# Attention stage of a four-layer graph network: pairs of 512-column tiles cast and subtracted as one, accumulators read behind the subtraction, degrees in three batches, drains replaced by semaphores

## The reference

```python
deg = jnp.clip(adj.sum(axis=1), 1.0)
dis = deg ** (-0.5)
adj_norm = dis[:, None] * adj * dis[None, :]
diffusion = adj_norm @ x - x
norms = jnp.maximum(jnp.linalg.norm(x, axis=-1), COS_EPS)
sim = x @ x.T / (norms[:, None] * norms[None, :])
attn = jax.nn.softmax(beta * sim * adj, axis=1)
return diffusion + jax.nn.sigmoid(alpha) * (attn @ x - x)
```

## Time and profile before

| | |
|---|---|
| median of 3 runs | 945.01 us (944.57 to 945.73) |
| profiled execution | 945.11 us, of which the span of its instructions 943.3 us |
| PE busy | 856.4 us (91%) |
| DVE busy | 642.5 us (68%) |
| ACT busy | 485.7 us (51%) |
| POOL busy | 292.1 us (31%) |
| attention stage | about 54 to 433 us of the span |

### The profile page before, as it was taken

How to read it: one execution, slowest core, us unless ns; L and a number is a source line. 1 busy time by engine, 2 the same in 40 slices (tenths; PEclk the granted TensorE clock), 3 DMA queues, 4 the chain that set the end, 5 groups by cost and what they waited for, 6 DMA issues and landing times.

```text
span 943.3 us, 18224 instructions
## 1 busy us (share of the span) xinstructions
PE 856.4 (91%) x6496; PEld 509.7 (54%) x6496; DVE 642.5 (68%) x1782; ACT 485.7 (51%) x1020; POOL 292.1 (31%) x380
## 2 busy tenths in 40 slices
PE   0189999999999999979999999999999999999992
PEld 0157676767676767645444445555455555545451
DVE  6989999999999999994344423322135676646576
ACT  5758687878687877653122212111026646525344
POOL 4665454544344544432111210000012222212121
PEclk9999999999999999999999999999999999999996
DMA  8848887988798989200000000000000000000100
GB/s 248 241 125 261 203 247 222 237 226 263 199 251 208 246 224 236 62 1 1 1 1 1 1 1 1 1 1 1 1 1 1 1 1 1 1 1 13 34 23 23
DMA packets 84813, 89.75 MB, mean 95 GB/s; under 512 B 71296, under 2 KB 76544, under 8 KB 76544
## 3 DMA queue, kind: packets, MB, share of 16 engines
q1 hardware_dynamic: 81088, 88.09, 33.7%
q10 hardware_dynamic: 3648, 0.61, 0.4%
HBM read 69.81 MB, written 2.10 MB: 76 GB/s over the span
## 4 chain that ended last, share of the span: by engine, by line
PE 53%; DVE 25%; issue 10%; POOL 4%; DVEq 3%; ACT 2%; DMA 1%; ACTq 0%; POOLq 0%; SPq 0%
PE ps_acc L1234 27%; PE ps_acc L1166 10%; DVE e_parts L762 6%; PE ps_s L1149 6%; DVE ps_s L756 4%; PE ps_t L1234 3%; PE ps_t L1149 3%; POOL att_sb L356 2%; DVE ps_t L756 2%; PE ps_s L1297 1%; DVE ez L689 1%; POOL e_parts L332 1%; PE ps_s L1265 1%; ACT ez L480 1%; DVE x L779 1%
## 5 line engine op out<-in xcount | busy, mean ns | idle before, releaser
L332 POOL CAST e_parts<-ez 128x512 f16<-128x512 f32 x256 | 158.0, 644 | 201.7 <-ACT ez L480 201.7
L1166 PE MATMUL ps_acc<-h_a,e_parts 128*128 128x129 f16 x3072 | 198.6, 220 | 21.6 <-DVE e_parts L762 20.8
L1166 PEld LDWEIGHTS ps_acc<-h_a,e_parts 128*128 128x128 f16 x3072 | 183.7, 97 | 61.4 <-DVE e_parts L762 33.1
L1234 PE MATMUL ps_acc<-adj_t,stage 128*128 128x512 fp8e4 x896 | 198.9, 379 | 0.0
L762 DVE TENSOR_TENSOR e_parts<-ez,e_parts 128x512 f16<-128x512 f32 x256 | 178.3, 735 | 10.3 <-POOL e_parts L332 9.5
L1234 PE MATMUL ps_acc<-adj_t,h_a 128*128 128x512 fp8e4 x768 | 170.3, 379 | 0.0
L434 ACT ACTIVATE bytes<-stage 128x1024 uint8<-128x1024 f32 x128 | 134.1, 1048 | 28.1 <-DMA stage<-in_adj 28.0
L1234 PEld LDWEIGHTS ps_acc<-adj_t,stage 128*128 128x128 f16 x896 | 87.1, 98 | 98.9
L1149 PE MATMUL ps_s<-u_t 128*128 128x512 f16 x516 | 127.0, 383 | 0.0
L480 ACT ACTIVATE ez<-ps_s,scal 128x1024 f32<-128x1024 f32 x86 | 103.1, 1199 | 42.4 <-DVE ps_s L756 40.7
L518 ACT ACTIVATE ez<-x,small 128x128 f32 (+1 forms) x96 | 39.5, 482 | 158.9 <-DVE small L881 158.9
(11 more groups left out here) (164 smaller groups left out, 830.8 us busy)
## 6 DMA issues: line engine op xcount, KB each, us to landing
stage<-in_adj SPq DMA_DIRECT2D x64, 1024.0 KB, 5.7
x<-in_x SPq DMA_DIRECT2D x4, 512.0 KB, 8.3
out<-x SPq DMA_DIRECT2D x8, 256.0 KB, 2.2
adj_t<-bytes SPq DMA_TRANSPOSE x64, 3.1
kernel_sb<-in_L_gnn_kernel ACTq DMA_DIRECT2D x1, 64.0 KB, 7.1
w_sb<-in_L_gnn_W ACTq DMA_DIRECT2D x1, 64.0 KB, 8.1
embed_top<-in_L_gnn_embed ACTq DMA_DIRECT2D x1, 64.0 KB, 8.2
embed_top<-in_L_gnn_layer ACTq DMA_DIRECT2D x1, 64.0 KB, 7.4
```

Of the source, the lines that this page charges most:

```text
L332: g.tensor_copy(e_parts[:, HI, g_s % RING, :], ez[:, g_s % RING, :]).then_inc(ehi_done, 1)
L1166: last = t.matmul(att_acc[:, b, 0:D + 1], e_parts[:, re, g_s % RING, P * b:P * (b + 1)], h_a[:, s, rh, 0:D + 1], start=(s == 0 and n == 0 ...
L1234: last = t.matmul(acc, h[:, k, r, :], adj_f8[:, k // 2, CW * c:CW * (c + 1), k % 2], start=(k == 0 and r == LO), stop=(k == NB - 1 and r = ...
```

## The change

- `high_part` becomes `high_pair`: one CAST of 1024 columns for two tiles. `low_part` becomes `low_pair`: one subtraction of 1024 columns. PE waits once for a pair instead of once for a tile.
- In iteration p the subtraction of p now stands ahead of `att_evac`. That reads the accumulators in PSUM with two instructions: the reciprocal of the sums, and a copy of the 512 columns which is scaled by the gate on the way. `att_tail` is left with four updates of x.
- The drains of `x_minus_h`, `att_evac` and `att_tail` are replaced by waits on semaphores (`x_less`, `x_att`, `acc_free`); one drain is added behind the last `att_tail`.
- `degrees` runs three times (for 4, 3 and 1 chunks) instead of eight, with the scaling of the sum folded into the clamp; POOL's eight roots are put at given pairs of chunks 4 to 7. ACT waits once, at pair 100, for all `x_minus_h`.

```diff
+DEGREES_AT = {(4, 8): (0, 4), (6, 8): (4, 7), (7, 5): (7, 8)}
+ROOT_AT = {(4, 9): 0, (4, 11): 1, (4, 13): 2, (5, 1): 3, (6, 9): 4, (6, 11): 5, (6, 13): 6,
+           (7, 6): 7}
...
-            def high_part(g_s):
-
-                if g_s % 2 == 0:
-                    pool.wait_ge(exp_done, g_s // 2 + 1)
-                if g_s >= RING:
-                    pool.wait_ge(e_used, g_s - RING + 1)
-                g.tensor_copy(e_parts[:, HI, g_s % RING, :], ez[:, g_s % RING, :]
+            def high_pair(p):
+
+                pool.wait_ge(exp_done, p + 1)
+                if p >= 2:
+                    pool.wait_ge(e_used, 2 * p - 2)
+                at = 2 * p % RING
+                g.tensor_copy(e_parts[:, HI, at:at + 2, :], ez[:, at:at + 2, :]
                               ).then_inc(ehi_done, 1)
...
+                if p + CAST_AHEAD == 2 * HPC * (NCH - 1):
+                    act.wait_ge(x_less, NCH)
...
                 v.scalar_tensor_tensor(pairs(x[:, blocks, :]), h0f[:, c, :, :], x_coef,
-                                       pairs(x[:, blocks, :]), ALU.mult, ALU.add)
-                dve.drain()
+                                       pairs(x[:, blocks, :]), ALU.mult, ALU.add
+                                       ).then_inc(x_less, 1)
...
-            def low_part(g_s):
-
-                dve.wait_ge(ehi_done, g_s + 1)
-                v.tensor_tensor(e_parts[:, LO, g_s % RING, :], ez[:, g_s % RING, :],
-                                e_parts[:, HI, g_s % RING, :], ALU.subtract).then_inc(elo_done, 1)
+            def low_pair(p):
+
+                dve.wait_ge(ehi_done, p + 1)
+                at = 2 * p % RING
+                v.tensor_tensor(e_parts[:, LO, at:at + 2, :], ez[:, at:at + 2, :],
+                                e_parts[:, HI, at:at + 2, :], ALU.subtract).then_inc(elo_done, 1)
 
             def att_evac(c):
 
                 dve.wait_ge(e_used, NB * (c + 1))
-                v.tensor_copy(att_sb[:, :, :], att_acc[:, :, 0:D + 1]).then_inc(acc_free, 1)
-                dve.drain()
+                if c:
+                    dve.wait_ge(x_att, c)
+                v.reciprocal(rec, att_acc[:, :, D]).then_inc(acc_free, 1)
+                v.tensor_scalar(att_sb[:, :, 0:D], att_acc[:, :, 0:D], sig_h, None, ALU.mult
+                                ).then_inc(acc_free, 1)
 
             def att_tail(c):
 
-                v.reciprocal(rec, att_sb[:, :, D])
-                dve.drain()
-                v.tensor_scalar(rec, rec, sig_h, None, ALU.mult)
-                dve.drain()
+                dve.wait_ge(acc_free, 2 * (c + 1))
+
+                dve.wait_ge(x_less, min(c + 2, NCH))
                 for b in range(BC):
                     xb = x[:, BC * c + b, :]
-                    v.scalar_tensor_tensor(xb, att_sb[:, b, 0:D], rec[:, b:b + 1], xb,
-                                           ALU.mult, ALU.add)
-                dve.drain()
...
+                    last = v.scalar_tensor_tensor(xb, att_sb[:, b, 0:D], rec[:, b:b + 1], xb,
+                                                  ALU.mult, ALU.add)
+                last.then_inc(x_att, 1)
...
                 if p + 1 < PAIRS:
                     z_pair(p + 1)
+                low_pair(p)
                 if c and k == 0:
                     att_evac(c - 1)
-                low_part(2 * p)
-                low_part(2 * p + 1)
...
-                if k == (5 if c == NCH - 1 else 8):
-                    degrees(c)
+                if (c, k) in DEGREES_AT:
+                    degrees(*DEGREES_AT[c, k])
...
-                    pe.wait_ge(acc_free, c)
-                pe.wait_ge(elo_done, g_s + 1)
+                    pe.wait_ge(acc_free, 2 * c)
+                if s % 2 == 0:
+                    pe.wait_ge(elo_done, g_s // 2 + 1)
```

More of the change, by code:

```diff
@@ L190, in program @@
                  "h_sq_in n_h_ok v_sq_in n_v_ok h2_sq_in n_h2_ok a_sq_in n_a_ok cat_sq_in "
-                 "n_cat_ok tanh_in tanh_out ln_in ln_out h2_ok v_ok v_out split_g diag_hi diag_ok").split()
+                 "n_cat_ok tanh_in tanh_out ln_in ln_out h2_ok v_ok v_out split_g diag_hi diag_ok "
+                 "x_less x_att").split()
         adj_in = [sem("adj_in0"), sem("adj_in1")]
@@ L201, in program @@
          n_cat_ok, tanh_in, tanh_out, ln_in, ln_out, h2_ok, v_ok, v_out, split_g, diag_hi,
-         diag_ok) = (
+         diag_ok, x_less, x_att) = (
             sem(n) for n in names)
@@ L324, in _ @@
                 low_h(q)
-            def high_part(g_s):
-                if g_s % 2 == 0:
-                    pool.wait_ge(exp_done, g_s // 2 + 1)
-                if g_s >= RING:
-                    pool.wait_ge(e_used, g_s - RING + 1)
-                g.tensor_copy(e_parts[:, HI, g_s % RING, :], ez[:, g_s % RING, :]
+            def high_pair(p):
[4 more added lines that the diff above has]
+                g.tensor_copy(e_parts[:, HI, at:at + 2, :], ez[:, at:at + 2, :]
                               ).then_inc(ehi_done, 1)
             def root_degree(c):
-                pool.wait_ge(pow_in, c + 1)
+                pool.wait_ge(pow_in, 1 if c < 4 else 2 if c < 7 else 3)
                 power(dis[:, BC * c:BC * (c + 1)], neg_half).then_inc(pow_ok, 1)
             for c in range(NCH):
[L341 to L346, removed]
+                for k in range(NP):
+                    high_pair(NP * c + k)
+                    if (c, k) in ROOT_AT:
+                        root_degree(ROOT_AT[c, k])
+            pool.wait_ge(pow_in, 4)
             power(d2, neg_half).then_inc(pow_ok, 1)
@@ L477, in exp_pair @@
                 if p >= 2:
[L478 removed]
+                    act.wait_ge(elo_done, p - 1)
                 at = 2 * p % RING
@@ L541, in _ @@
             act.wait_ge(s_done, PAIRS)
-            act.wait_ge(pow_in, NCH + 1)
+            act.wait_ge(pow_in, 4)
             for m in (0, 1):
@@ L757, in z_pair, with degrees @@
                                 .rearrange("p i t -> p t i"), ALU.mult).then_inc(z_done, 1)
[L759 to L763 removed]
+            def low_pair(p):
[3 more added lines that the diff above has]
+                                e_parts[:, HI, at:at + 2, :], ALU.subtract).then_inc(elo_done, 1)
             def att_evac(c):
                 dve.wait_ge(e_used, NB * (c + 1))
[L768 to L769 removed]
+                if c:
[3 more added lines that the diff above has]
+                                ).then_inc(acc_free, 1)
             def att_tail(c):
[L773 to L776 removed]
+                dve.wait_ge(acc_free, 2 * (c + 1))
+                dve.wait_ge(x_less, min(c + 2, NCH))
                 for b in range(BC):
                     xb = x[:, BC * c + b, :]
[L779 to L786 removed]
+                    last = v.scalar_tensor_tensor(xb, att_sb[:, b, 0:D], rec[:, b:b + 1], xb,
+                                                  ALU.mult, ALU.add)
+                last.then_inc(x_att, 1)
+            def degrees(first, end):
+                cut = slice(BC * first, BC * end)
+                dve.wait_ge(cast_done, HPC * end)
                 v.tensor_reduce(deg[:, cut], deg_parts[:, cut, :], mybir.AxisListType.X,
@@ L789, in degrees @@
                 dve.drain()
-                v.tensor_scalar(deg[:, cut], deg[:, cut], 1.0 / A_BYTE, None, ALU.mult)
-                dve.drain()
-                v.tensor_scalar(dis[:, cut], deg[:, cut], 1.0, None, ALU.max
+                v.tensor_scalar(dis[:, cut], deg[:, cut], 1.0 / A_BYTE, 1.0, ALU.mult, ALU.max
                                 ).then_inc(pow_in, 1)
@@ L837, in _ @@
             att_tail(NCH - 1)
+            dve.drain()
             for m in rest:
```

6 lines of the change are left out of this document (3 added, 3 removed).

## The result

| | before | changed |
|---|---|---|
| median, measured side by side | 945.37 us (944.57 to 946.26, 4 runs) | 937.14 us (937.08 to 938.30, 4 runs) |
| profiled execution, its span | 945.11, 943.3 | 937.08, 935.3 |
| mean of the six chunks of the earlier trace rows | 45.68 | 44.34 |

The ratio is 0.9916, with a 95% interval of 0.9898 to 0.9933: 8.2 us less by the medians, where 6.7 were forecast.

A forecast was written before the change was run, and what follows sets the result against it. PE's pace plus its border waits bound the kernel, with the staging loop close behind. Gains of 1.54 us a chunk less 0.5, times seven borders, give 7.3; less 0.6 at the end, 938.4 us; range 930.5 to 946.5.

The forecast's parts named there:

- What bounds the kernel: In the six attention chunks: PE's 42.7 us of a chunk's 45.68, plus 2.96 of waits, mostly two at the border.
- Accumulators behind the subtraction: At a chunk's border, the subtraction fills DVE's 0.90 us idle before the accumulators are read: 0.97 us gained.
- Tail: DVE's updates of x one pair after the border: slot shrinks from 2.37 to 2.16 us, gain 0.21 a chunk.
- the drain of `x_minus_h`: The drain behind `x_minus_h` costs its gap and lost overlap; removing it gains 0.16 us a chunk.
- the collision: In the tail, POOL's next CAST falls between the updates and holds them some 1.12 us.
- staging loop: ACT's casts waiting for stage loads: two buffers allow chunks of about 44.1 us, so at most 1.56 us saved each.
- Wide CAST and subtraction at nothing, the later handover once: Costed at nothing, hidden by PE's 2.67 us a pair; PE gets pairs 0.60 us later, paid once.
- The handover at the end: End of the last chunk: PE starts behind the whole subtraction, 0.6 us later.
- Degrees: DVE's 0.56 us of degrees a chunk, five of eight gone: between 0 and 0.56, taken as 0.2 a chunk.
- What the staging loop takes back: Late staged quarters at each border take 0.5 us of the 1.54 gained a chunk, leaving 1.04.
- The staging floor of 44.1 a chunk: Two waits for the stage 11.03 us apart for four pairs, so two staging buffers allow about 44.1 us a chunk.
- The rival that ended at this floor: Faster still: without the CAST holding updates, borders save 1.56 us each, 934.8 us; chance 0.20, shared with reaching PE's pace.

The follow-up runs named there:

- e1: Kernel before, with only the order changed: at a chunk's border both 512-column subtractions stand ahead of the copy of the accumulators; 941.35 us, ratio 0.9958.
- e2: Kernel before, with only the 1024-column CAST and subtraction and PE's one wait per pair; 950.34 us, ratio 1.0050.
- e3: Kernel before, with only accumulators read in PSUM, tail of four updates and semaphores for drains; reading still ahead of the narrow subtractions; 941.68 us, ratio 0.9961.
- e6: Changed kernel without copy and later tail: reciprocal, gate and four updates of x directly from PSUM behind the first wide subtraction; 932.02 us, ratio 0.9839.
- e12: As e6, but the gate is multiplied to the sums as read from PSUM, ahead of the reciprocal; 931.24 us, ratio 0.9839.
- e9: Changed kernel with 512-column CASTs and subtractions again, PE waiting once for a tile; 937.51 us, ratio 0.9914.
- e4: Changed kernel with the accumulators read ahead of a chunk's first wide subtraction again; 942.94 us, ratio 0.9972.
- e8: Changed kernel with degrees and their roots once in each chunk again, folded scaling kept; 937.32 us, ratio 0.9906.
- e5: Changed kernel with only 2 of the 64 adjacency loads, later casts rereading the same staged halves; 932.37 us, ratio 0.9844.
- e13: As e12, with CASTs and subtractions for single tiles again; 929.35 us, ratio 0.9837.
- e7: Changed kernel with SP issuing the next load ahead of the transposing DMA instead of behind it; 938.07 us, ratio 0.9910.

## Why the prediction was right

The time (938.4 forecast, 937.14 measured), its sign and its mechanism hold. Its terms were less good than their sum, and that the sum came so near is in part luck.

- **What bounds the kernel.** Right: PE's pace and its waits at the border. The idle time ahead of the products moves with the time in all three single parts: −4.4 (e1), +5.3 (e2), −4.9 (e3), where the times moved by −4.3, +4.7 and −4.0. It is not a full account, though: the whole change takes 5.6 off it and 8.2 off the time. Over the six chunks PE's idle time fell by 6.0 us and its busy time by 2.1 (260.92 to 258.83), so that some waiting may stand in the matmul rows themselves; in e3 the 24 products at 147.78 take 1.78 us, and others 1.53 to 1.56.
- **Accumulators behind the subtraction**, 0.97 a border of which the stage was to take back 0.5. Right: DVE idles 0.27 (under 0.3 was asked for). Forecast was thus 0.47 a border net; alone it gives 4.3 / 7 = 0.61, undone it costs 5.3 / 7 = 0.76.
- **Tail**, 0.21, and the drain of `x_minus_h`, 0.16. Mis-sized: together they measure 4.0 / 7 = 0.57 in e3. The CAST came first and held one update, as forecast, but for some 0.8 us (342 to at most 1182 ns) and not 1.12. The wide CAST takes 1.04 us where nothing holds it (e6), and 1.16 here. By the Trainium skill's "SBUF — State Buffer", section "Who interferes with whom", a VectorE instruction with two SBUF inputs contends with a GpSimd one that reads SBUF, and one with at most one SBUF input, outside the two-port modes, does not. These holds agree with it, and so do e12's four updates, which take one operand from PSUM and 1.13 us beside a CAST. Beside this term the prediction says that without the collision the sum would grow by 7 × 1.12 = 7.8; by its own staging loop it could have grown by 0.52 a chunk at most (1.56 − 1.04).
- **Wide CAST and subtraction at nothing, the later handover once.** Right for the kernel as changed (e9), but not for the reason given. The later handover is paid at each border where DVE is last, 0.65 us in e2, so PE's own 2.67 us a pair does not hide it. With the new tail most of that price is gone already in the old order (e4 against e3), and none is left in the new one (e9); how the tail does it is not shown.
- **The handover at the end**, 0.6. Mis-sized: from the start of the third pair's products in the last chunk to PE's last wait it is 39.33 us before and 39.12 in the changed kernel, 38.79 in e9. The width costs 0.33 there, and as much again at the start of the stage, for which the prediction has no term: the first products start at 61.33 us, and at 60.98 in e9.
- **Degrees**, 0.2 a chunk. Wrong: nothing (e8). The prediction's own lower bound held: in the earlier trace rows they ran while a stage load was late anyway.
- **What the staging loop takes back**, 0.5 a chunk. Right in kind, too small: a chunk takes 44.34 with the loads and 43.66 without them (e5), so 0.68. What stands ahead of it was put too low as well: without loads a chunk is 45.68 − 43.66 = 2.02 below that of before, where the terms say 1.54 (the kernel before was not run without loads). Both together make 1.34 a chunk and not 1.04.
- **The sum.** Up to PE's last wait of the stage the change gains 8.92 us, where 6.7 were forecast, and 0.9 is lost in later layers, for which the prediction has no term. The two errors partly cancel.
- **The staging floor of 44.1 a chunk.** Wrong. It was taken from two waits 11.03 us apart, which are the pace at which that kernel ran; chunks of 43.66 and 43.38 run with all loads. The rival that ended at this floor, at 934.8, is passed with all loads by e12 (931.24) and e13 (929.35).

Left open: what decides in which chunks a late cast reaches PE, and what the tail has to do with the width and with the later layers.

## What to carry to other kernels

When an engine waits for the last operation of a stage, put ahead of that operation's reader whatever is already ready and is wanted next: here it gave 4 to 5 us with two lines exchanged. Making an instruction twice as wide also makes its first result twice as late; price that at each place where the consumer is waiting, not in the steady state. Here it cost 4.7 us on the kernel before and nothing measurable on the changed one. And the distance between two waits for a buffer is not that buffer's floor, because the waiting loop is also paced by the others.

## What the runs showed of the hardware

- A CAST of 1024 columns on GpSimd takes 1.04 us where nothing holds it (e6); two of 512 take 1.17.
- A TENSOR_SCALAR of 128 x 4 numbers from SBUF to SBUF, 0.23 us at some borders of e6, takes 0.90 and 1.07 at others, and 1.08 in e2, where a CAST runs. A RECIPROCAL of that size takes 0.18 beside a CAST (e12).
- Exchanging a load and a transposing DMA on one queue moved 33 us of waits from the one to the other, and the time not at all (e7).
